# Alternating PSUM bank pairs in two loops of a two-layer transformer kernel

## The reference

```python
x = x + L0_attn(layernorm(x))     # 16 heads of 64, causal, latent projections
x = x + L0_ffn(layernorm(x))      # quantized linear 1024 -> 1024
x = x + L1_attn(layernorm(x))     # 16 heads, causal, latent of 256
x = x + L1_ffn(layernorm(x))      # 1024 -> 4096 -> 1024, with a sin in between
# inside L0_ffn, x being the normed input:
a_scale = max(abs(x), axis=-1) + 1e-8             # one value per token
a_quant = round(clip(x / a_scale * 127, -128, 127))
y = einsum('bsi,oi->bso', a_quant, w_quant) * (w_scale * a_scale / 127)
# inside L1_attn, x being the normed input:
c_kv = x @ W_dkv.T                                # T x 256
q    = (x @ W_dq.T @ W_uq.T)                      # T x 256, then T x 1024
```

## Time and profile before

| | |
|---|---|
| Four runs, us | 7587.43, 7599.73, 7602.05, 8025.59 |
| Their median, us | 7600.89 |
| Profiled execution, us | 7591.8 |
| Its span on the slowest core (core 4), us | 7590.3 |
| Spans of the eight cores, us | 7578.3 to 7590.3 |
| Mean granted TensorE clock of the cores | 0.854 to 0.857 |
| Busy, share of the span | PE 78%, DVE 30%, ACT 27%, POOL 8% |

### The profile page before, as it was taken

How to read it: one execution, slowest core, us unless ns; L and a number is a source line. 1 busy time by engine, 2 the same in 40 slices (tenths; PEclk the granted TensorE clock), 3 DMA queues, 4 the chain that set the end, 5 groups by cost and what they waited for, 6 DMA issues and landing times.

```text
span 7590.3 us, 100698 instructions; the slowest of 8 cores (7578.3 to 7590.3 us)
## 1 busy us (share of the span) xinstructions
PE 5912.8 (78%) x15346; PEld 2157.4 (28%) x15346; DVE 2247.8 (30%) x3468; ACT 2046.5 (27%) x3044; POOL 634.1 (8%) x580
## 2 busy tenths in 40 slices
PE   6888988889863223678978998889678879789796
PEld 2333333333321001222322232223223323223232
DVE  1333223331204675121121111111233332342323
ACT  1333333333310001002322322223342341432420
POOL 0000000000002432000000000000020120210200
PEclk8888988889985556888988988899889989899896
DMA  1000000000011000000000000000012212122121
GB/s 55 1 1 1 1 1 1 1 1 1 1 38 52 1 0 10 8 1 1 1 7 1 1 1 1 1 1 1 17 60 73 68 59 84 56 68 73 62 73 67
DMA packets 58427, 179.36 MB, mean 24 GB/s; under 512 B 9723, under 2 KB 16294, under 8 KB 57894
## 3 DMA queue, kind: packets, MB, share of 16 engines
q1 hardware_dynamic: 57894, 172.92, 6.9%
HBM read 164.44 MB, written 8.39 MB: 23 GB/s over the span
## 4 chain that ended last, share of the span: by engine, by line
PE 68%; DVE 15%; issue 8%; ACT 4%; DMA 2%; POOL 1%; DVEq 1%; ACTq 0%; SPq 0%; POOLq 0%
PE PS L341 17%; PE PS L359 16%; PE PS L1323 11%; PE PS L1259 7%; DVE R__98 L924 2%; DVE W1L L1225 2%; PE PS L347 2%; PE PS L366 2%; PE PS L285 2%; ACT W1H L1223 1%; DVE B__99 L921 1%; PE PS L280 1%; PE PS L1008 1%; PE PS L1023 1%; PE PS L968 1%
## 5 line engine op out<-in xcount | busy, mean ns | idle before, releaser
L353 ACT ACTIVATE E<-PS,SM 128x512 f32<-128x512 f32 x1280 | 863.7, 685 | 1362.1 <-PE PS L347 683.9
L370 DVE COPY RBF<-PS 64x512 f32<-64x512 f32 x128 | 88.2, 689 | 2253.6 <-PE PS L366 2236.6
L341 PE MATMUL PS<-QP,KHD 64*128 64x512 f32 x1280 | 746.1, 675 | 10.7 <-issue 10.6
L359 PE MATMUL PS<-E,VFB 128*128 128x512 f32 x1280 | 659.7, 611 | 4.9 <-ACT E L353 4.9
L359 PE MATMUL PS<-E,VFA 128*128 128x512 f32 x1280 | 656.7, 611 | 1.3 <-ACT E L353 1.3
L1259 PE MATMUL PS<-XNH,W1H 128*128 128x512 bf16 x1024 | 438.6, 428 | 186.0 <-ACT W1H L1223 148.1
L1259 PE MATMUL PS<-XNH,W1L 128*128 128x512 bf16 x1024 | 437.7, 427 | 117.6 <-DVE W1L L1225 107.3
L1291 POOL TENSOR_TENSOR SC<-SC 128x512 f32<-128x512 f32 x128 | 161.6, 1263 | 3498.7 <-PE PS L1259 3453.7
L1259 PE MATMUL PS<-XNL,W1H 128*128 128x512 bf16 x1024 | 433.9, 424 | 0.4 <-DVE XNL L1207 0.2
L1323 PE MATMUL PS<-ACH,W1H 128*128 128x512 bf16 x1024 | 389.5, 380 | 33.8 <-ACT ACH L1302 33.6
L1323 PE MATMUL PS<-ACL,W1H 128*128 128x512 bf16 x1024 | 389.5, 380 | 9.4 <-POOL ACL L1309 5.6
(11 more groups left out here) (235 smaller groups left out, 6779.2 us busy)
## 6 DMA issues: line engine op xcount, KB each, us to landing
W1F<-w1p SPq DMA_DIRECT2D x128, 512.0 KB, 3.5
W2F<-w SPq DMA_DIRECT2D x128, 512.0 KB, 3.5
TM<-x_in SPq DMA_DIRECT2D x16, 512.0 KB, 13.3
WTR<-w0T SPq DMA_DIRECT2D x16, 512.0 KB, 3.8
y_out<-XO SPq DMA_DIRECT2D x16, 512.0 KB, 2.6
WPA<-wo1T SPq DMA_DIRECT2D x16, 256.0 KB, 2.6
WPA<-wuq SPq DMA_DIRECT2D x8, 128.0 KB, 2.0
WPB<-wuk SPq DMA_DIRECT2D x8, 128.0 KB, 2.0
```

Source lines behind the costliest of these rows:

```text
L341: e.matmul(s.PS[sb][:], k_lhsT(kc), q_rhs(qq), start=True, stop=not diag),
L353: e.activation(s.E32[eb][:], s.PS[sb][:], AF.Exp, bias=negc),
L359: e.matmul(pvbank[:], v_lhsT(kc), s.E32[eb][:], start=(kc == 0), stop=(kc == kcmax - 1)),
```

## The change

In both loops the banks alternate from turn to turn. In the first loop the even blocks use PS4 and PS5, the odd blocks PS6 and PS7 as before. In the second loop the even windows use PS2 to PS5 as before, the odd windows PS0 and PS1 for the W_dq products and PS6 and PS7 for the W_dkv products. The instructions that read the banks follow. No instruction is added, removed or put in another place of its engine's list, and no SBUF tile changes.

```diff
         for tt in range(16):
+            ab = 4 + 2 * (tt % 2)
             for grp in range(2):
-                bk = f"PS{6 + grp}"
-                bank = s.PS[6 + grp]
+                bk = f"PS{ab + grp}"
+                bank = s.PS[ab + grp]
...
-                 e.tensor_reduce(AMX[:, tt:tt + 1], s.PS[6][:], AX.X, OP.max,
+                 e.tensor_reduce(AMX[:, tt:tt + 1], s.PS[ab][:], AX.X, OP.max,
                                  apply_absolute_value=True),
-                 r=("PS6",), w=("AMXa",))
+                 r=(f"PS{ab}",), w=("AMXa",))
...
-                 e.tensor_reduce(AMX[:, 32 + tt:33 + tt], s.PS[7][:], AX.X, OP.max,
-                                 apply_absolute_value=True),
-                 r=("PS7",), w=("AMXb",))
+                 e.tensor_reduce(AMX[:, 32 + tt:33 + tt], s.PS[ab + 1][:], AX.X,
+                                 OP.max, apply_absolute_value=True),
+                 r=(f"PS{ab + 1}",), w=("AMXb",))
...
         for qq in range(NQ):
+            ub = 2 if qq % 2 == 0 else 0
+            cb = 4 if qq % 2 == 0 else 6
             for c in range(NCH):
                 s.xn_into(s.SC[0][:], "SC0", c, qq)
                 for m in range(2):
-                         e.matmul(s.PS[2 + m][:],
+                         e.matmul(s.PS[ub + m][:],
...
-                         e.matmul(s.PS[4 + m][:],
+                         e.matmul(s.PS[cb + m][:],
...
-                     e.tensor_copy(UU[m][:, QW * qq:QW * (qq + 1)], s.PS[2 + m][:]),
-                     r=(f"PS{2 + m}",), w=(f"UU{m}",))
+                     e.tensor_copy(UU[m][:, QW * qq:QW * (qq + 1)], s.PS[ub + m][:]),
+                     r=(f"PS{ub + m}",), w=(f"UU{m}",))
...
-                     e.tensor_copy(CKV[m][:, QW * qq:QW * (qq + 1)], s.PS[4 + m][:]),
-                     r=(f"PS{4 + m}",), w=(f"CKV{m}",))
+                     e.tensor_copy(CKV[m][:, QW * qq:QW * (qq + 1)], s.PS[cb + m][:]),
+                     r=(f"PS{cb + m}",), w=(f"CKV{m}",))
```

More of the change, by code:

```diff
@@ L841, in emit_l0f @@
                 s.close_group(bk)
-            s.do("vector", lambda e, tt=tt, AMX=AMX:
-                 e.tensor_reduce(AMX[:, tt:tt + 1], s.PS[6][:], AX.X, OP.max,
+            s.do("vector", lambda e, tt=tt, AMX=AMX, ab=ab:
+                 e.tensor_reduce(AMX[:, tt:tt + 1], s.PS[ab][:], AX.X, OP.max,
                                  apply_absolute_value=True),
-                 r=("PS6",), w=("AMXa",))
-            s.do("vector", lambda e, tt=tt, AMX=AMX:
-                 e.tensor_reduce(AMX[:, 32 + tt:33 + tt], s.PS[7][:], AX.X, OP.max,
-                                 apply_absolute_value=True),
-                 r=("PS7",), w=("AMXb",))
+                 r=(f"PS{ab}",), w=("AMXa",))
+            s.do("vector", lambda e, tt=tt, AMX=AMX, ab=ab:
+                 e.tensor_reduce(AMX[:, 32 + tt:33 + tt], s.PS[ab + 1][:], AX.X,
+                                 OP.max, apply_absolute_value=True),
+                 r=(f"PS{ab + 1}",), w=("AMXb",))
             s.do("vector", lambda e, tt=tt, AMX=AMX:
@@ L966, in emit_l1a @@
                 for m in range(2):
-                    s.do("tensor", lambda e, c=c, m=m:
-                         e.matmul(s.PS[2 + m][:],
+                    s.do("tensor", lambda e, c=c, m=m, ub=ub:
+                         e.matmul(s.PS[ub + m][:],
                                   WA[0][:, 256 * c + 128 * m:256 * c + 128 * (m + 1)],
                                   s.SC[0][:], start=(c == 0), stop=(c == NCH - 1)),
-                         r=("WA0", "SC0"), w=(f"PS{2 + m}",))
-                    s.do("tensor", lambda e, c=c, m=m:
-                         e.matmul(s.PS[4 + m][:],
+                         r=("WA0", "SC0"), w=(f"PS{ub + m}",))
+                    s.do("tensor", lambda e, c=c, m=m, cb=cb:
+                         e.matmul(s.PS[cb + m][:],
                                   WA[1][:, 256 * c + 128 * m:256 * c + 128 * (m + 1)],
                                   s.SC[0][:], start=(c == 0), stop=(c == NCH - 1)),
-                         r=("WA1", "SC0"), w=(f"PS{4 + m}",))
-            s.close_group("PS2", "PS3", "PS4", "PS5")
+                         r=("WA1", "SC0"), w=(f"PS{cb + m}",))
+            s.close_group(f"PS{ub}", f"PS{ub + 1}", f"PS{cb}", f"PS{cb + 1}")
             for m in range(2):
-                s.do("vector", lambda e, m=m, qq=qq:
-                     e.tensor_copy(UU[m][:, QW * qq:QW * (qq + 1)], s.PS[2 + m][:]),
-                     r=(f"PS{2 + m}",), w=(f"UU{m}",))
-                s.do("vector", lambda e, m=m, qq=qq:
-                     e.tensor_copy(CKV[m][:, QW * qq:QW * (qq + 1)], s.PS[4 + m][:]),
-                     r=(f"PS{4 + m}",), w=(f"CKV{m}",))
+                s.do("vector", lambda e, m=m, qq=qq, ub=ub:
+                     e.tensor_copy(UU[m][:, QW * qq:QW * (qq + 1)], s.PS[ub + m][:]),
+                     r=(f"PS{ub + m}",), w=(f"UU{m}",))
+                s.do("vector", lambda e, m=m, qq=qq, cb=cb:
+                     e.tensor_copy(CKV[m][:, QW * qq:QW * (qq + 1)], s.PS[cb + m][:]),
+                     r=(f"PS{cb + m}",), w=(f"CKV{m}",))
         s.loadw("wuq1T", WUQT, "WUQT", cols=1024)
```

## The result

The changed kernel was measured at 7862.06 us, the median of seven executions (7658.58 to 8035.50), beside 7828.25 us for ten of the kernel before (7587.43 to 8045.19). The comparison over the executions with the least lowered clocks gave a ratio of 1.0115, with a 95% interval of 1.0059 to 1.0170: slower by its interval, and the median is above the predicted range. That ratio is the mean of only two executions of the changed kernel (7658.58 and 7704.52 us) over the mean of the four fastest of the kernel before (7587.43 to 7602.05).

The account below looks back on a forecast made before the run. PE was taken to wait in both loops for chunks made by DVE, not for banks. All terms summed to 0 us, so 7591.8 us like the profiled execution, or 7600 us against the median; range 7578 to 7618 us.

Parts of the forecast that it names:

- What bounds the loops: Both loops: at a hand-over PE waits for DVE to make the next chunk, not for a bank to be read.
- What the instructions wait for: Hand-overs of both loops: waits left on DVE's semaphore keep their value; 15 by 0 us and 3 by 0 us.
- The number of waits: Moved PE instructions in both loops: each waits on the same semaphores as before; 0 us.
- the bound of 9.8 us: Both loops: one 0.051 us wait more or less on 64 transposes and 128 matmuls, either way; chance 4%, inside "same".
- How fast another bank is: Moved accesses in both loops: other banks are about equally fast; differences at most 0.1 us for copies, 0.2 us for the rest.
- The faster rival: Hand-overs of both loops: evacuating a bank comes to lie beside PE's next work, saving 33 us, so 7568 us; chance 3%.
- The slower rival: Second loop: TensorE's clock falls, 29 more chunks take 8.25 us each, costing 41 us, so 7642 us; chance 3%.
- How the numbers follow: Closing step for the whole kernel: chances faster 0.04, same 0.92, slower 0.04; time 7600 us, range 7578 to 7618 us.

Follow-up runs that it names:

- the two later comparisons: The changed kernel measured again without an edit, twice, each against the kernel before: ratios 1.0004 and 0.9987.
- the order with its tiles: Against the kernel before, chunks made ahead of the bank readers, in more tiles; ratio 0.9861 with fixed banks, 7477.9 us on cores at 0.855 or more.

## Why the prediction was wrong, point by point

**What bounds the loops: right.** The idle times before lines 839 and 971 are those forecast, and so is what ends them.

**What the instructions wait for: right.** Two sums of 0 us were forecast, for 15 and for 3 hand-overs. Over all cores with a clock of 0.855 or more in the two later comparisons (each with the executions taken beside it), the changed kernel's median is 7583.7 us (95 cores) and that of the kernel before 7583.4 us (231): a change of 0.3 us.

**The number of waits: right.** 34073 wait instructions on PE's queue in both; the bound of 9.8 us was not needed. **How fast another bank is: right**, 690 to 692 ns for the reductions in any pair.

**The faster rival** did not occur, for the reason given: it took another order in DVE's list for PE to wait for a bank at all. Even then removing those waits gave 4.0 us in one loop and cost 5.8 us in the other. And its price of 33 us, counted from the hand-overs alone, says nothing of the 107 us that the order with its tiles brought. **The slower rival**, the clock in the second loop, did not occur there: that stretch has 0.85 in the changed kernel too.

**The step that failed**: the term of the sum for the clock of the execution was left at nothing, and the range went by it. It is in "How the numbers follow": the range was built on "the lower runs' spread (7587 to 7602)". The fourth run, 8025.59 us, stood in the table and was left aside without a price, as if it could not be the rule. It was: of the changed kernel's first seven executions none was free of a lowered clock, and they took 59 to 436 us more than 7600. The kernel before, measured beside it, had a median of 7828.25 us over ten, which misses the range of 7578 to 7618 as well. The missing term was the clock of the execution, in stages that the change does not touch: 265 us in layer 0's attention on one core, 53.5 us in layer 1's attention on another. And the sentence that 0.2% can be told from no change holds only between executions without it: the two with the lowest times that the first comparison rested on (7658.58 and 7704.52 us) had cores 0 to 3 at 7587.2 us or less, and cores 4 and 5, which set the time, at a clock of 0.837 to 0.847. (Cores 6 and 7 had 0.838 to 0.844 and took 7581.3 to 7591.0 us: a lowered clock that fell where it costs nothing would look like that, but no profile of these two executions shows where it fell.) The ratio of 1.0115 is that of cores 4 and 5 to undisturbed ones, and not that of the two kernels; the two later comparisons of the same kernel, 1.0004 and 0.9987, enclose 1.

**What stays open** is what lowers the clock, and why on some cores and in some stages; no experiment here reaches it.

## What to carry to other kernels

Before giving a loop a second pair of banks, look at which instruction ends PE's wait at the hand-over, and where that instruction stands in its engine's list: if it is a maker of data that stands behind the readers of the bank, the bank is free before PE can use it, and what helped here was another order in the list together with more tiles for the data (1.4%). Count also the waits inside a turn, and not only those at the hand-over. A removed wait can be replaced by another: here PE waited for data instead, whose making took DVE 8.9 us longer, so fixed banks may be as good even then. When a measured ratio contradicts a trace that is the same instruction for instruction, look at the span and granted clock of every core before looking for a mechanism, and compare stages from their own first instruction to the next one's: a window that is cut at fixed times puts a loss into whatever stage comes last.

## What the runs showed of the hardware

- A lowered clock comes in part of an execution. In layer 0's attention on core 0 of the first profile, the f32 score matmuls of 128x512 lasted 698 ns (median) where they last 592 otherwise; layer 1's score matmuls on the same core had their usual median of 589 to 590 ns, and that core's clock from the first loop on was 0.85. The unchanged kernel shows it too (0.77 on core 2 in the last profile of it, with a median of 698 ns).
- What it costs depends on the stage: 265 us in layer 0's attention at 0.76 in place of 0.89, nothing in layer 1's feed-forward part at 0.76 in place of 0.90, where the bf16 matmuls of line 1262 lasted 437 ns in place of 377.
- Cores go in pairs: in that execution cores 0 and 1 took 7850.6 and 7860.5 us, cores 2 and 3 7640.2 and 7640.4, with nearly one mean clock for all four (0.811 to 0.817).
- A small DVE subtraction or multiplication of 128x128 f32 took 0.29 us alone and mostly 0.47 to 0.54 us beside POOL's like instructions; POOL's subtractions took 0.50 in place of 0.45 us, its multiplications 0.45 us either way.
